# An S4D layer: ScalarE issues the stores of a finished channel behind its copy of the states

## The reference

```python
dtA = (-exp(log_A_real) + 1j * A_imag) * exp(log_dt)[:, None]
K = 2.0 * einsum('hn,hnl->hl', Cs, exp(dtA[:, :, None] * arange(L))).real
u_m = x * mask
y = irfft(rfft(u_m, 2 * L) * rfft(K, 2 * L))[..., :L] + u_m * D[:, None]
out = x + y * mask
```

## Time and profile before

| | |
|---|---|
| Time, median of 3 runs | 870.07 us |
| The profiled execution's own time | 868.06 us |
| Its span | 866.3 us |
| Mean granted TensorE clock | 0.994 of full speed |
| PE busy | 819.3 us (95%) |
| DVE busy | 738.2 us (85%) |
| ACT busy | 618.1 us (71%) |
| POOL busy | 636.8 us (74%) |
| DMA queue q1, share of 16 engines | 69.2% |

### The profile page before, as it was taken

How to read it: one execution, slowest core, us unless ns; L and a number is a source line. 1 busy time by engine, 2 the same in 40 slices (tenths; PEclk the granted TensorE clock), 3 DMA queues, 4 the chain that set the end, 5 groups by cost and what they waited for, 6 DMA issues and landing times.

```text
span 866.3 us, 22503 instructions
## 1 busy us (share of the span) xinstructions
PE 819.3 (95%) x6168; PEld 755.1 (87%) x6168; DVE 738.2 (85%) x2030; ACT 618.1 (71%) x1713; POOL 636.8 (74%) x690
## 2 busy tenths in 40 slices
PE   0568999999999999999999999999999999999997
PEld 0457998999999999999998999999999999999996
DVE  8957988888888888888888888888888888888886
ACT  2546776777777777777777777777777777777774
POOL 3746777777777787777777878787878787878771
PEclk9979999999999999999999999999999999999999
DMA  5023777877777777677777777777776777777775
GB/s 109 0 62 91 191 192 177 192 186 192 188 198 183 193 188 196 185 196 184 195 186 194 185 193 188 192 189 193 188 193 188 194 188 194 188 193 189 196 189 133
DMA packets 161236, 152.72 MB, mean 176 GB/s; under 512 B 13376, under 2 KB 161088, under 8 KB 161088
## 3 DMA queue, kind: packets, MB, share of 16 engines
q1 hardware_dynamic: 161216, 152.48, 69.2%
HBM read 84.08 MB, written 67.30 MB: 175 GB/s over the span
## 4 chain that ended last, share of the span: by engine, by line
PE 88%; DVE 3%; DMA 3%; ACT 2%; SPq 2%; issue 1%; DVEq 0%
PE y L938 13%; PE y L940 13%; PE y L939 13%; PE y L976 12%; PE v L955 10%; PE xt_even L926 6%; PE xt_odd L926 6%; PE v L938 3%; PE v L939 3%; PE v L940 3%; DMA xall<-in_x_dram 3%; PE y L933 2%; PE y L934 2%; PE y L1045 1%; DVE q L669 1%
## 5 line engine op out<-in xcount | busy, mean ns | idle before, releaser
L497 ACT ACTIVATE room<-v 64x192 f32<-64x192 f32 (+1 forms) x768 | 235.8, 307 | 174.8 <-DVE v L842 156.9
L842 DVE SCALAR_TENSOR_TENSOR v<-v,RV,mid 128x192 f32<-128x192 f32 (+2 forms) x512 | 192.5, 376 | 57.1
L842 DVE SCALAR_TENSOR_TENSOR mid<-room,RV,v 128x192 f32<-128x192 f32 (+2 forms) x512 | 184.5, 360 | 42.6 <-ACT room L497 23.1
L938 PE MATMUL y<-thi,uhi 128*128 128x256 f32 x512 | 186.4, 364 | 0.0
L838 DVE COPY_PREDICATED xall<-mask,y 128x512 f32<-128x512 int32 x256 | 176.0, 736 | 1.6 <-issue 1.6
L938 PE MATMUL y<-fhi,zhi 128*128 128x256 f32 x512 | 154.6, 302 | 0.8 <-DVE zlo L642 0.8
L940 PE MATMUL y<-thi,ulo 128*128 128x256 f32 x512 | 144.5, 282 | 0.0
L940 PE MATMUL y<-fhi,zlo 128*128 128x256 f32 x512 | 144.0, 281 | 0.0
L939 PE MATMUL y<-tlo,uhi 128*128 128x256 f32 x512 | 144.0, 281 | 0.0
L939 PE MATMUL y<-flo,zhi 128*128 128x256 f32 x512 | 144.0, 281 | 0.0
L476 POOL TENSOR_TENSOR room<-W,B 128x512 f32 (+1 forms) x127 | 141.9, 1117 | 0.0
(11 more groups left out here) (167 smaller groups left out, 1938.6 us busy)
## 6 DMA issues: line engine op xcount, KB each, us to landing
xall<-in_x_dram SPq DMA_DIRECT2D x256, 256.0 KB, 4.6
out_dram<-xall SPq DMA_DIRECT2D x254, 256.0 KB, 3.4
traw<-krows SPq DMA_DIRECT2D x128, 128.0 KB, 3.0
xall<-B SPq DMA_DIRECT2D x2, 512.0 KB, 5.9
out_dram<-xall SPq DMA_DIRECT2D x4, 128.0 KB, 2.4
krows<-ksb SPq DMA_DIRECT2D x8, 1.0 KB, 2.0
krows<-ksb SPq DMA_DIRECT2D x8, 15.0 KB, 1.7
cin<-in_L_cond_C_dram SPq DMA_DIRECT2D x1, 64.0 KB, 1.9
```

The source lines that it names most:

```text
L497: return act.activation(dst, src, ACT.Copy)
L842: return dve.scalar_tensor_tensor(out=out, in0=src, scalar=RV[:, k:k + 1, h], in1=other, op0=ALU.mult, op1=ALU.add)
L938: pe.matmul(o, a_hi, b_hi, start=start, stop=False, skip_group_check=True)
```

## The change

`store` moves out of SP's stream to the top and takes the engine as an argument. In each slot from the second on, ACT waits for `s_pred` and issues the two stores of channel h-1, behind `z_high` and ahead of `x_high`. SP issues no stores any more but those of the last channel, which it still stores in two halves. Sizes, buffers and the counts on the semaphores stay as they are.

```diff
+        def store(eng, g, j, m=slice(0, CPH)):
+            for f in range(2):
+                eng.dma_start(o_v[chan(g, j), f, :, m],
+                              xs[j][f * B:(f + 1) * B, :].rearrange("p (m t) -> p m t", t=CHUNK)[:, m]
+                              ).then_inc(s_out[j], 16)
+
         block = ctx.enter_context(nc.Block())
@@ the sync engine
-            def store(g, j, m=slice(0, CPH)):
-                for f in range(2):
-                    sp.dma_start(o_v[chan(g, j), f, :, m],
-                                 xs[j][f * B:(f + 1) * B, :].rearrange("p (m t) -> p m t", t=CHUNK)[:, m]
-                                 ).then_inc(s_out[j], 16)
@@ its slot
-                if exists(g, j, -1):
-                    sp.wait_ge(s_pred, 2 * h)
-                    store(*on(g, j, -1))
@@ behind its slots
-                store(*last, slice(part * CPH // 2, (part + 1) * CPH // 2))
+                store(sp, *last, slice(part * CPH // 2, (part + 1) * CPH // 2))
@@ ScalarE, its slot
                 if has0:
                     z_high(*here)
+                if has0 and exists(g, j, -1):
+                    act.wait_ge(s_pred, 2 * chan(g, j))
+                    store(act, *on(g, j, -1))
                 if has2:
                     x_high(*two)
                     e_high(*two)
```

## The result

The changed kernel takes 996.37 us, the median of 4 runs (994.26 to 997.15), against 871.13 us for the kernel before in 4 runs (869.45 to 874.89): a ratio of 1.144, 95% interval 1.1404 to 1.1476. The forecast was 1018 us, range 940 to 1080. The profiled execution has a span of 995.3 us at a granted clock of 0.992.

The account below looks back on a forecast made before the run. PE's own work was taken as the bound, at 6.22 us a slot; an ACT-DVE loop lengthened to 7.42 adds 1.20 us in 126 slots, 151 less 3, giving 1018 us, range 940 to 1080.

Parts of the forecast that it names:

- the ring: ACT and DVE, `turn_evens` through `turn_pairs` and `fours` to the next `turn_evens`: 6.03 us, about 0.19 of room, growing to 7.42.
- The six pieces: Stretches from `turn_evens` to the next: 2.14, 0.42, 1.57, 0.15, 1.71 and 0.04 us, together 6.03.
- The removed issues on SP: SP loses two store issues a slot, 1.51 us; relief worth 0 to 0.7 us, taken as 0.
- The added wait: ACT's wait for `s_pred` behind `z_high`: met over 0.9 us before ACT comes to it, costs nothing.
- The added issues: Two store issues on ACT between `z_high` and `x_high`: 1.81 us from start to start in place of 0.42.
- The reason given for the size of an issue: Store issues on SP: duration goes with transfer size, 644 ns for 256 runs, 345 for 128.
- What is moved: Stores start earlier, loads of x go up some 2 us, landing takes 3.4 us; none of it a term.
- The first: Between `z_high` and `x_high`, the issues hardly hold ACT: PE stays the bound, 868 to 870 us; 10%.
- The second: Issues on ACT are shorter, 333 ns each: +0.36 us a slot, about 913 us; 8%.
- the third: Issues on ACT are dearer, behind the end of `z_high` (1086 us) or conflicting with SP's (1055 to 1095); 18%.
- The fourth: The granted clock falls since PE now pauses; would only add to the rest; 2%.
- One sign: PE's busy time was to stay, some 820 us in a span of 1010.

Follow-up runs that it names:

- e4: Kernel before, SP's stores kept, with two extra 128x512 copies on ACT behind the copy of the states; no DMA moved: 971.3 us, ratio 1.1176.
- e5: As e1, with three buffers for the Toeplitz row instead of two, its load issued at the slot's start: 868.75 us, ratio 1.0002 to the kernel before.
- e3: Changed kernel with each store cut in two: ACT issues the first halves, SP the second halves where it stored before: 989.92 us, ratio 1.1389.
- e8: As e3, but ACT's two stores have one run to a partition and SP's two have three: 954.86 us, ratio 1.0989.
- e1: Changed kernel with the wait and both stores behind `x_odd`, ACT's last copy of the slot, instead of behind `z_high`: 920.47 us, ratio 1.0611.
- run 119: Not a follow-up run: the text counts 119 of ACT's 254 issues, over the changed kernel's profiled run, that overlap one of SP's.
- e6: Changed kernel with the wait and both stores ahead of `z_high` instead of behind it: 986.6 us, ratio 1.1369.
- e7: Kernel before, all DMAs on SP, with the loads of x right behind the Toeplitz row's load and ahead of the stores: 977.71 us, ratio 1.1267.

## Why the prediction was right

**What bounds the kernel, and the ring.** Right. The six pieces read in one slot of before are there again after: 2.13 us to `zhi` (2.14 forecast), 1.51 from `uhi` to the end of `turn_pairs` (1.57), 0.14 to `fours` (0.15), 1.71 of `fours` and 0.04 to the next `turn_evens` (the same), and ACT's idle time ahead of `turn_evens` stayed 1.27. e4 shows the ring without any DMA, e5 that the same issues outside it are free.

**The removed issues on SP** are worth nothing that can be measured: e5 has them removed too and stands at 1.0002.

**The added wait** cost nothing where it stands: the second `choose` of the slot shown ends on DVE at 484.39 and the first store starts at 485.31.

**The added issues.** Right in kind, a little too dear. The pair took 1.42 us, where SP's row gave 1.51, and the arithmetic ahead of it, put at 0.2, lay before the start of `zhi`; the first store starts 0.05 behind it. So `zhi` to `uhi` was 1.59 and not 1.81. That is the term that was mis-sized, 0.22 us in a slot or some 28 us. The pieces from `turn_evens` to `zhi` and from `uhi` to `fours` were another 0.08 shorter, which gives the 7.12 of the slot shown. The other way went the slots around the hardware loop's jump, up to 7.54 us in place of 7.13, which I had left out and which lift the mean by some 0.1; together 7.23 for 7.42, and 996 for 1018. So a part of the nearness is luck: two errors went against each other.

**The reason given for the size of an issue was wrong**: e3 and e8 show that it does not go with the number of runs as I had it (644 ns for 256, 345 for 128). The trace of the kernel before already spoke against it: SP's last four stores, 64 partitions by two runs, took 596 to 622 ns there. The number was taken from the very same transfers, so the sum did not suffer.

**What is moved.** I wrote that none of the moved DMAs is a term. In the change itself this holds nearly: `thi` waited 8.6 us for the row in all, though it lands in 4.4 us, since the slot had become longer. It would have been wrong for a faster place: in e1 the landing alone costs 51 us.

**The rivals.** The first, that the issues hardly hold ACT, is ruled out where they stand by 1.06 us of idle time ahead of `uhi`. The second and the third are out by the 625 ns, and by the first store, which starts 0.05 us behind the start of `zhi` and not at its end. Issues on both sequencers at once did not lengthen them: in the slot shown ACT's pair runs until 486.73 (485.31 + 1.42), and SP's load of the row starts beside it at 486.57 and takes 0.34 us as ever. Over the run 119 of ACT's 254 issues overlap one of SP's, and their median is 0.62 us, as that of the other 135. The Trainium skill, Perfetto Trace Analysis, section DMA Instruction — HWDGE, has the sequencer held until the end of its issue; the trace of ACT agrees, `uhi` never starts before the second issue ends (0.05 to 0.15 us behind it, in 125 slots). Of the exclusive lock that this section describes these rows show no cost. The fourth is out: the granted clock was 0.992. One sign was read wrongly ahead: PE's busy time did not stay at 820 us but rose to 882, with the same 6168 matmuls; its largest groups have the same mean durations as before. Added up one by one, the matmuls last 1874 us before and 1891 after; what changed is that they overlap less, so that more of the span counts as busy.

## What to carry to other kernels

An engine's idle time is room only for work that stands behind the last thing that others wait for. So follow the ring from an instruction to its next turn, sum the pieces, and compare with the period, before calling 1.3 us of idle time free. On ACT here, a DMA issue held back what stands behind it in the program for its full 0.5 to 0.65 us, and nothing that stands ahead (e1, e5); but it was itself held by a copy ahead of it whose data had not come (e6). So put it behind the last copy that is urgent, ahead of a wait that is long anyway. When DMAs move, look for the small load that lands just in time: it was the first to be late. And look at what the issuing stream itself waits for at the new place: in e7 that wait became the bound.

## What the runs showed of the hardware that was not expected

- ACT's sequencer runs ahead of its copies, but not past one whose data are missing: in e1 a store was issued while five copies that stand ahead of it in the program (`ehi`, `eod`, two of `turn_pairs`, `x_odd`) had not started; in e6 the first store starts less than 0.2 us behind the landing of the row for which the copy ahead of it waits, in 85 of 127 slots.
- An issue took 625 ns with two runs of 256 floats to each of 64 partitions as with four, and 487 ns with one; on SP, 345 ns for one run to each of 128 partitions. Why is not shown.
- The landing of one 128 KB load rose from 3.0 us to between 3.7 (e8) and 5.4 (e5), with the same bytes moved in all. It stayed at 2.9 in e4, where no DMA is moved. In e3, e8 and e7, each time with the loads of x over 2 us behind it, stores issued less than 1 us ahead of it went with 4.2, 3.7 and 4.6 us.
- The issue of that load on SP lasted 727 ns in the median in e7, where SP's stores stand right ahead of it, and 345 before.
- The granted clock stayed between 0.985 and 0.996 in all these runs, with PE idle 1 us in each slot or not.
